# A two-layer graph network on one core: half of the zeroes begun in a later stage, one attention tile loaded earlier, and count masks spread over nine steps

## The chip, the cores and the metric

The kernel runs as one launch on one core of one Trainium2 chip. The metric is the device time of a run in microseconds. Three runs of the kernel before took 3403.36, 3404.73 and 3406.10 us; the median is 3404.73 us. One more run was profiled.

## The reference

Input is `x` (1250 nodes by 768) and 20,000 edges `src`, `dst`. Two layers follow, each a sum of a graph attention, a performer attention and a small feed-forward part:

```python
xn = _layernorm(x, axis=-1)
x = x + _L0_gnn_ref(xn, edge_index, ...) + _L0_mix_ref(xn[None], ...)[0]   # 2 GAT layers; performer + MLP
x = x + _L0_ffn_ref(_layernorm(x, axis=-1)[None], ...)[0]                  # routed experts
xn = _layernorm(x, axis=-1)
x = x + _L1_gnn_ref(xn, edge_index, ...) + _L1_mix_ref(xn[None], ...)[0]
x = x + _L1_ffn_ref(_layernorm(x, axis=-1)[None], ...)[0]
```

The graph attention is `e = leaky_relu(a_src[src] + a_dst[dst])`, a maximum of `e` over the edges that enter a node, `exp(e - m[dst])`, and a sum of `h[src]` with these weights over the edges. The kernel turns the edge list into a dense matrix of counts (how many edges lead from node s to node d), since an edge can occur more than once. The performer's output is `(phi(q) @ (phi(k).T @ v)) / (phi(q) @ sum(phi(k)))`, times a projection `proj_w`, plus a bias.

## The kernel before

Tokens are cut into `NT` = 10 tiles of `TP` = 125 rows. Float32 products run as three passes (`y_lo*w_hi`, `y_hi*w_lo`, `y_hi*w_hi`). The program is a row of stages. A stage is a `Stage` with an `nc.Block()`: each engine has its own instruction list, and lists are ordered only by semaphores. At the end of a block all engines meet (in the norm stage this is line 247), then the stage's semaphores are cleared (L68) and all engines meet again (L69). Nothing of the next stage is issued before. The order within a list is the order in which the Python code writes it; there is no scheduler.

The stages that matter here, in order:

- `norm_stage`. Rows of `x` come in, are normalised twice and turned. SP (the DMA queue's engine) stores the normalised rows to `xn_d`. POOL waits for the last rows of `x` (L276, `x_ld[4]`), and then `edges.clear` (L135) issues 26 DMAs that write zeroes over two count matrices `adj0_d` and `adj1_d` in HBM: 13 for each, 12 with rows and a small one for spare cells. Each matrix has 1250 x 1250 float32 cells, 6.25 MB.
- `performer_stage` "perf0" (six pairs of heads). DVE also finds the count of each edge's cell beside its own work (`counted.count`, L182), and POOL adds the counts into the matrices by 160 indirect DMAs (`counted.add`, L200 to L216), in turn to `adj0_d` and `adj1_d`, so that each waits for the one two before it to land. The first waits until all zeroes have landed (`edges.cleared`, L206). The first weights of this stage are loaded in the norm stage; its next ones (`load_v(0)`, features, `load_qk(1)`) are issued by SP in the stage.
- `gat_project_stage` "gat00proj". In step t, PE turns tile t+1 of the rows, multiplies tile t in two halves of the columns (c = 0, 1; 18 matmuls each), and after each half turns one half tile of the counts (`turn_counts`, L1718), of which DVE makes a bfloat16 mask (`keep_mask`, L1900). q = 2s + c names the half tiles of matrix rows s, 20 in all. The sum of `adj0` and `adj1` for rows s is `add_counts(s)` on DVE (L1895). All turned things pass through two PSUM banks `tps` in turn: an entry of the list `turns` may be written only when the one two entries before it has been read by DVE (`wait_slot`, L1711). In step t the halves 2t-2 and 2t-1 are turned, and 18 and 19 behind the last step. SP stores tile t of `h` as soon as it is kept, and behind the last of these the whole mask in three pieces (L1674).
- `proj_stage` ("proj0" and, in layer 2, "proj1"). SP loads tile 0 of the attention's output, the six blocks of the projection's weights, tile 1, the bias, rows for tiles 0 and 1, then the other tiles (L1077 to L1088). PE turns tile 0 and tile 1, and only then multiplies tile 0 (`turn_tile`, L1118), block by block as ACT and DVE have split the weights. POOL adds the bias to the rows (L1211), which come in pieces of tiles 0-1, 2-4 and 5-9; DVE adds PE's product to that (L1255).

Of the kernel before, what the change touches and what calls it, by code (L numbers as in the profile page):

```python
# [21 lines left out]
NT = 10  # L22
# [94 lines left out]
class Edges:  # L117
# [17 lines left out]
    def clear(self, pool):  # L135
        for flat in self.adj_flat:
            for r0 in range(0, N, ROWS):
                rn = min(ROWS, N - r0)
                pool.dma_start(flat[r0 * N:(r0 + rn) * N].rearrange("(p a n) -> p a n", p=rn, a=2),
                               self.zero[0:rn, :].unsqueeze(1).to_broadcast([rn, 2, N // 2])).then_inc(self.cleared, 16)  # L140
                self.cleared_n += 16
            pool.dma_start(flat[N * N:N * N + EXTRA].rearrange("(a n) -> a n", a=1),
                           self.zero[0:1, 0:EXTRA]).then_inc(self.cleared, 16)
            self.cleared_n += 16
# [17 lines left out]
class EdgeCounts:  # L162
# [37 lines left out]
    def add(self, pool):  # L200
        edges, added, sets = self.edges, self.added, len(self.edges.adj_flat)
        pool.wait_ge(edges.cleared, edges.cleared_n)
# [15 lines left out]
def norm_stage(nc, ident, src, dst, lower, edges, eps, x_d, normed_d, gain_cols, shift_cols, yT, first, late):  # L218
# [6 lines left out]
    with Stage(nc, "norm") as S:  # L225
# [21 lines left out]
        with nc.Block() as block:  # L247
# [25 lines left out]
            def _(pool):  # L273
# [4 lines left out]
                edges.clear(pool)  # L278
# [730 lines left out]
def proj_stage(nc, name, ident, attn_d, w_d, bias_d, xn_d, x_d, sum_d, eps, gain, shift, yT, ahead=(), more_shift_d=None,  # L1009
# [19 lines left out]
    with Stage(nc, name) as S:  # L1029
# [34 lines left out]
        with nc.Block() as block:  # L1064
            @block.sync
            def _(sp):
# [10 lines left out]
                load_a(0)  # L1077
                for kb in range(KB):
                    load_w(kb)
                load_a(1)  # L1080
# [499 lines left out]
def gat_project_stage(nc, name, ident, x_d, k, act_kind, bias_d, w_d, heads, width, asrc_d, adst_d, h, a_s, a_d, rows_d,  # L1580
# [12 lines left out]
    with Stage(nc, name) as S:  # L1593
# [30 lines left out]

        turns = [("x", 0), ("x", 1)]
        for t in range(1, NT):
            turns += [("x", t + 1)] if t + 1 < NT else []
            turns += [("m", 2 * t - 2), ("m", 2 * t - 1)] if edges is not None else []
        turns += [("m", 2 * NT - 2), ("m", 2 * NT - 1)] if edges is not None else []
# [11 lines left out]
        with nc.Block() as block:  # L1641
# [69 lines left out]
            def _(pe):  # L1711
# [35 lines left out]
                for t in range(NT):  # L1747
# [6 lines left out]
                    for c in range(2):  # L1754
# [10 lines left out]
                        if edges is not None and t:  # L1765
                            turn_counts(2 * t - 2 + c)
                if edges is not None:
                    turn_counts(2 * NT - 2)
                    turn_counts(2 * NT - 1)
# [61 lines left out]
            def _(dve):  # L1831
# [86 lines left out]
                dve.wait_ge(att_ld, 64)  # L1918
                for t in range(NT):
# [7 lines left out]
                    if edges is not None and t >= 2:  # L1927
                        keep_mask(2 * t - 4)
                    if t >= 2:
                        terms(t - 2)  # L1930
                    if edges is not None and t:
                        add_counts(t - 1)
                        if t >= 2:
                            keep_mask(2 * t - 3)
# [4 lines left out]
                if edges is not None:  # L1939
                    keep_mask(2 * NT - 4)  # L1940
                    add_counts(NT - 1)
                    keep_mask(2 * NT - 3)
                terms(NT - 2)
                if edges is not None:
                    keep_mask(2 * NT - 2)
                    keep_mask(2 * NT - 1)
# [1937 lines left out]
```

## Time and profile before

| | before |
|---|---|
| median of three runs | 3404.73 us (3403.36 to 3406.10) |
| profiled execution, whole | 3403.53 us |
| its span (first to last instruction) | 3401.4 us |
| busy: PE / PEld / DVE / ACT / POOL | 84 / 74 / 69 / 43 / 16 % |
| norm stage to perf0 | 0 to 84 us |
| perf0 | 84 to 549 us |
| gat00proj | 549 to 690 us |
| proj0, first instruction on SP | 690.60 us |

The profile is of one execution. It gives busy times and start times per instruction, and for each idle time what ended it. POOLq and SPq are the sequencers of these engines: DMA issues and waits that take no time on the engine. The span leaves out what lies before the first and behind the last instruction, 2.1 us here.

### The profile page before, as it was taken

What the parts mean: (1) busy time and instruction counts of PE and PEld (TensorE: products, weight loads), DVE (VectorE), ACT (ScalarE), POOL (GpSimd) and SP (SyncE); (2) the same over time, 40 slices, a digit from 0 to 9 for tenths busy, and PEclk for the clock granted to TensorE, in tenths of its full rate; (3) what the DMA queues carried; (4) which work ended last, traced back from release to release, by engine and by line L of the source; (5) the groups of instructions that cost most, each with busy time, mean ns of one, the idle gap of its engine ahead of it and who ended that gap; (6) DMA issues with size and microseconds to landing.
All of it is one profiled execution on the core that took longest, in us unless ns stands there. A gap on an engine that the chain in (4) does not pass through costs nothing. (4 is left out here: it accounts for less than half of the span.)

```text
span 3401.4 us, 50787 instructions
## 1 busy us (share of the span) xinstructions
PE 2869.5 (84%) x17896; PEld 2528.3 (74%) x17896; DVE 2332.3 (69%) x4168; ACT 1460.6 (43%) x2436; POOL 530.0 (16%) x358
## 2 busy tenths in 40 slices
PE   1999997877999997887997599878999977887795
PEld 1999996766888997777896233247999977777794
DVE  4765642856842544998664888657788868998775
ACT  3464652222112332554243577521556522554345
POOL 2677783220000000000002300000000022000000
PEclk9999998988999998999998699979999988998897
DMA  8433326684213554523131311253311068213301
GB/s 263 84 51 57 47 22 155 215 206 111 67 44 87 174 165 118 140 67 84 29 75 48 80 42 43 55 165 119 77 41 51 23 174 224 76 46 79 85 21 47
DMA packets 254534, 319.48 MB, mean 94 GB/s; under 512 B 98467, under 2 KB 176804, under 8 KB 254206
## 3 DMA queue, kind: packets, MB, share of 16 engines
q1 hardware_dynamic: 176574, 272.11, 29.8%
q0 software_dynamic: 77760, 44.83, 6.5%
q8 instruction: 110, 1.80, 0.2%
q14 instruction: 90, 0.74, 0.1%
HBM read 236.35 MB, written 79.53 MB: 93 GB/s over the span
## 5 line engine op out<-in xcount | busy, mean ns | idle before, releaser
L210 POOL DMA_INDIRECT adj_d<-edge_val,edge_off x160 | 336.3, 2102 | 150.8 <-DMA adj_d<-edge_val,edge_off 59.2
L3274 DVE TENSOR_TENSOR expert_wgel<-expert_gel,expert_wps 128x417 f32<-128x417 f32 (+1 forms) x384 | 202.8, 584 | 57.0 <-PE expert_wps L3199 47.3
L2185 PE MATMUL gat00att_ops<-gat00att_h,gat00att_p 125*125 x1600 | 198.8, 280 | 50.4 <-DVE gat00att_p L2159 50.4
L2185 PE MATMUL gat10att_ops<-gat10att_h,gat10att_p 125*125 x1600 | 195.9, 279 | 47.1 <-DVE gat10att_p L2159 47.1
L2185 PEld LDWEIGHTS gat00att_ops<-gat00att_h,gat00att_p 125*125 125x125 f32 x1600 | 184.7, 190 | 64.6 <-issue 64.5
L2185 PEld LDWEIGHTS gat10att_ops<-gat10att_h,gat10att_p 125*125 125x125 f32 x1600 | 184.0, 192 | 59.1 <-issue 59.1
L3246 ACT ACTIVATE expert_gel<-expert_hps 128x417 f32<-128x417 f32 (+1 forms) x384 | 193.8, 519 | 63.7 <-DVE expert_wgel L3274 52.3
L596 PE MATMUL perf_wide<-y_lo,perf_qk_hi 128*128 128x416 f32 (+1 forms) x432 | 155.5, 360 | 44.6 <-DVE perf_qk_lo L780 44.0
L734 ACT ACTIVATE xn_room<-perf_wide,perf_lnm 125x384 f32<-125x384 f32 (+2 forms) x228 | 114.2, 622 | 158.5 <-PE perf_wide L620 85.6
L1358 PE MATMUL fc_ps<-y_lo,fc_w_hi 128*128 128x512 f32 (+1 forms) x432 | 154.6, 358 | 21.4 <-DVE fc_w_lo L1400 21.4
L1511 PE MATMUL fc_ops<-fc_w_hi,fc_x_lo 128*125 128x384 f32 x480 | 163.7, 341 | 7.1 <-DVE fc_w_lo L1563 7.1
L1511 PE MATMUL fc_ops<-fc_w_lo,fc_x_hi 128*125 128x384 f32 x480 | 163.3, 340 | 0.0
L1511 PE MATMUL fc_ops<-fc_w_hi,fc_x_hi 128*125 128x384 f32 x480 | 162.8, 339 | 0.0
L1358 PE MATMUL fc_ps<-y_hi,fc_w_lo 128*128 128x512 f32 (+1 forms) x432 | 155.0, 359 | 0.0
L1358 PE MATMUL fc_ps<-y_hi,fc_w_hi 128*128 128x512 f32 (+1 forms) x432 | 154.8, 358 | 0.0
L596 PE MATMUL perf_wide<-y_hi,perf_qk_lo 128*128 128x416 f32 (+1 forms) x432 | 153.6, 356 | 0.0
L596 PE MATMUL perf_wide<-y_hi,perf_qk_hi 128*128 128x416 f32 (+1 forms) x432 | 153.4, 355 | 0.0
L2106 ACT ACTIVATE gat00att_e<-gat00att_e,a_s 125x1250 f32<-125x1250 f32 x80 | 107.0, 1338 | 105.2 <-DVE gat00att_e L2144 105.0
L2106 ACT ACTIVATE gat10att_e<-gat10att_e,a_s 125x1250 f32<-125x1250 f32 x80 | 107.0, 1338 | 97.0 <-DVE gat10att_e L2144 96.8
L2943 POOL MEMSET first_z<- 3x1250 bf16 x2 | 2.2, 1136 | 906.2 <-POOLq L69 906.2
L3192 PE MATMUL expert_hps<-first_z,first_w 99*128 99x417 bf16 (+1 forms) x384 | 134.3, 353 | 9.6 <-SPq L3143 8.6
L3199 PE MATMUL expert_wps<-first_wp,first_spread 128*128 128x417 f16 (+1 forms) x384 | 134.7, 352 | 5.6 <-DVE expert_wgel L3274 5.6
(503 smaller groups left out, 8281.1 us busy)
## 6 DMA issues: line engine op xcount, KB each, us to landing
fc_w<-in_L_mix_fc_w SPq DMA_DIRECT2D x96, 384.0 KB
adj_d<-edge_zero POOLq DMA_DIRECT2D x22, 546.9 KB, 28.0
gat00proj_adj<-adj_d POOLq DMA_DIRECT2D x20, 546.9 KB, 8.2
edge_keys<-keys_d SPq DMA_DIRECT2D x20, 437.5 KB
gat00att_sh<-shift_d SPq DMA_DIRECT2D x16, 546.9 KB
sh<-shift_d SPq DMA_DIRECT2D x16, 546.9 KB
perf_w<-in_L_mix_qkv_w SPq DMA_DIRECT2D x18, 384.0 KB
perf_w<-in_L_mix_W_qkv SPq DMA_DIRECT2D x18, 384.0 KB
```

The lines of the kernel that those rows point to most:

```text
L210: edges.nc.gpsimd.indirect_dma_start(out=edges.adj_flat[u].rearrange("(n a) -> n a", a=1), out_offset=bass.IndirectOffsetOnAxis(ap=edges.o ...
L596: ins = pe.matmul(wide[:, c, 0:cn], qk_parts[wp][:, 1 - side, kb, :], y_parts[yp][:, kb, c0:c0 + cn], start=(kb == 0 and n == 0), stop=(kb ...
L734: act.activation(out, in_, ACT.Exp, bias=lnm[0:parts, 0:1], scale=scale).then_inc(exp_done, 1)
L1358: ins = pe.matmul(ps[:, u, c0:c0 + cn], wp[:, u, kb, :], yT[yp][:, kb, c0:c0 + cn], start=(kb == 0 and n == 0), stop=(kb == KB - 1 and n = ...
L1511: ins = pe.matmul(ops[0:TP, t % 4, c * 512:c * 512 + half], xp[:, u, rows], wp[:, u, c * half:(c + 1) * half], start=(k == 0 and n == 0), ...
L2106: act.activation(e[:, s % RING, :], e[:, s % RING, :], ACT.Exp, bias=a_s02[:, bass.ds(hd, 1), s]).then_inc(e_done, 1)
L2185: ins = pe.matmul(ops[0:TP, u, b, t * w:(t + 1) * w], p[:, s, (t0 + t) * TP:(t0 + t + 1) * TP], h[:, s, bass.ds(hd, 1), :], start=(s == 0 ...
L2943: nc.gpsimd.memset(first.z[len(NPART) * ER:ZK, u, :], 1.0).then_inc(first_set, 1)
L3192: pe.matmul(hps[:, q % 3, 0:cn], w1[0:ZK, u, j * 128:(j + 1) * 128], z[0:ZK, u, c0:c0 + cn], start=True, stop=True).then_inc(h_done, 1)
L3199: pe.matmul(wps[:, q % 3, 0:cn], spread[:, j, :], wp[:, u, c0:c0 + cn], start=True, stop=True).then_inc(w_done, 1)
L3246: act.activation(gel[:, q % 3, 0:cn], hps[:, q % 3, 0:cn], ACT.Gelu_apprx_tanh).then_inc(gel_done, 1)
L3274: dve.tensor_tensor(wgel[:, q % W, 0:cn], gel[:, q % 3, 0:cn], wps[:, q % 3, 0:cn], ALU.mult).then_inc(wgel_done, 1)
```

## The change

Three things are changed.

1. `clear` takes a list of matrices. The norm stage clears `adj_flat[0:1]`; `add` in perf0 begins with `edges.clear(pool, edges.adj_flat[1:])` and then waits for all zeroes.
2. In `proj_stage`, `load_a(1)` is issued before the six `load_w`. This holds for proj0 and proj1.
3. In gat00proj the 20 half tiles of the counts are dealt over steps 1 to 9 by a list `due`: two in each step and three in steps 4 and 7, none behind the last step. Sums of the two matrices move with them.

```diff
-    def clear(self, pool):
-        for flat in self.adj_flat:
+    def clear(self, pool, flats):
+        for flat in flats:
...
     def add(self, pool):
         edges, added, sets = self.edges, self.added, len(self.edges.adj_flat)
+        edges.clear(pool, edges.adj_flat[1:])
         pool.wait_ge(edges.cleared, edges.cleared_n)
...
-                edges.clear(pool)
+                edges.clear(pool, edges.adj_flat[0:1])
...
                 load_a(0)
+                load_a(1)
                 for kb in range(KB):
                     load_w(kb)
-                load_a(1)
...
+        due, halves = [[]], iter(range(2 * NT))
+        for t in range(1, NT):
+            due.append([next(halves) for _ in range(3 if t in (4, 7) else 2)])
...
-            turns += [("m", 2 * t - 2), ("m", 2 * t - 1)] if edges is not None else []
-        turns += [("m", 2 * NT - 2), ("m", 2 * NT - 1)] if edges is not None else []
+            turns += [("m", q) for q in due[t]] if edges is not None else []
...
                         if edges is not None and t:
-                            turn_counts(2 * t - 2 + c)
+                            for q in (due[t][1:] if c else due[t][0:1]):
+                                turn_counts(q)
                 if edges is not None:
-                    turn_counts(2 * NT - 2)
-                    turn_counts(2 * NT - 1)
                     pe.wait_ge(mask_kept, 2 * NT)
...
+                pending = []
                 for t in range(NT):
...
-                    if edges is not None and t >= 2:
-                        keep_mask(2 * t - 4)
+                    if edges is not None and pending:
+                        keep_mask(pending.pop(0))
                     if t >= 2:
                         terms(t - 2)
                     if edges is not None and t:
-                        add_counts(t - 1)
-                        if t >= 2:
-                            keep_mask(2 * t - 3)
+                        for q in due[t]:
+                            if q % 2 == 0:
+                                add_counts(q // 2)
+                        for q in pending:
+                            keep_mask(q)
+                        pending = list(due[t])
+                        if len(pending) > 2:
+                            keep_mask(pending.pop(0))
...
-                if edges is not None:
-                    keep_mask(2 * NT - 4)
-                    add_counts(NT - 1)
-                    keep_mask(2 * NT - 3)
                 terms(NT - 2)
                 if edges is not None:
-                    keep_mask(2 * NT - 2)
-                    keep_mask(2 * NT - 1)
+                    for q in pending:
+                        keep_mask(q)
                 terms(NT - 1)
```

On POOL, the zeroes stand in the norm stage before the change (L139 and L142 are the DMAs of `clear`, L247 the end of the block, L210 the indirect adds of perf0):

```order
L139 DMA adj_d<-edge_zero 224x1x625 x11
L139 DMA adj_d<-edge_zero 36x1x625
L142 DMA adj_d<-edge_zero 16x1x8
L139 DMA adj_d<-edge_zero 224x1x625 x11
L139 DMA adj_d<-edge_zero 36x1x625
L142 DMA adj_d<-edge_zero 16x1x8
L247 UNCONDITIONAL_BRANCH
L68 ISA
L490 UNCONDITIONAL_BRANCH
L210 DMA adj_d<-edge_val,edge_off 1562628x1 x160
```

And on POOL after the change (its lines are numbered one higher there):

```order
L139 DMA adj_d<-edge_zero 224x1x625 x11
L139 DMA adj_d<-edge_zero 36x1x625
L142 DMA adj_d<-edge_zero 16x1x8
L248 UNCONDITIONAL_BRANCH
L68 ISA
L491 UNCONDITIONAL_BRANCH
L139 DMA adj_d<-edge_zero 224x1x625 x11
L139 DMA adj_d<-edge_zero 36x1x625
L142 DMA adj_d<-edge_zero 16x1x8
L211 DMA adj_d<-edge_val,edge_off 1562628x1 x160
```

Thirteen of the 26 zero DMAs have moved behind the end of the norm stage and stand directly before the first add.

On DVE in gat00proj, steps 4 and 5 before the change (L1869 is `low`, L1904 `keep_mask`, L1838 and L1843 `terms`, L1897 `add_counts`):

```order
L1869 TENSOR_TENSOR gat00proj_xT_lo<-gat00proj_tps,gat00proj_xT_hi 128x750
L1904 TENSOR_SCALAR gat00proj_mask<-gat00proj_tps 125x5x125
L1838 TENSOR_TENSOR gat00proj_prod<-gat00proj_h,gat00proj_att 125x1024 x2
L1843 TENSOR_REDUCE a_s<-gat00proj_prod 125x8
L1843 TENSOR_REDUCE a_d<-gat00proj_prod 125x8
L1897 TENSOR_TENSOR gat00proj_adj<-gat00proj_adj 125x1250
L1904 TENSOR_SCALAR gat00proj_mask<-gat00proj_tps 125x5x125
L1869 TENSOR_TENSOR gat00proj_xT_lo<-gat00proj_tps,gat00proj_xT_hi 128x750
L1904 TENSOR_SCALAR gat00proj_mask<-gat00proj_tps 125x5x125
```

And the same steps on DVE after the change (lines two higher):

```order
L1871 TENSOR_TENSOR gat00proj_xT_lo<-gat00proj_tps,gat00proj_xT_hi 128x750
L1906 TENSOR_SCALAR gat00proj_mask<-gat00proj_tps 125x5x125
L1840 TENSOR_TENSOR gat00proj_prod<-gat00proj_h,gat00proj_att 125x1024 x2
L1845 TENSOR_REDUCE a_s<-gat00proj_prod 125x8
L1845 TENSOR_REDUCE a_d<-gat00proj_prod 125x8
L1899 TENSOR_TENSOR gat00proj_adj<-gat00proj_adj 125x1250 x2
L1906 TENSOR_SCALAR gat00proj_mask<-gat00proj_tps 125x5x125 x2
L1871 TENSOR_TENSOR gat00proj_xT_lo<-gat00proj_tps,gat00proj_xT_hi 128x750
L1906 TENSOR_SCALAR gat00proj_mask<-gat00proj_tps 125x5x125
```

Step 4 has one sum and one mask more. The mask behind the second L1871 is of half 7 now; it was of half 6 before. On PE the five transposes of `gat00proj_adj` that close steps 4 and 7 have become ten, and the fifteen that close step 9 have become five.

## Rows read from the trace of the kernel before

**Rows 1.** Window: PE, PEld, DVE, ACT, POOL busy us, clock, DMA share, GB/s

```profile
58.00:82.00 24.00, 0.00 (x0) 0.00 (x0) 0.00 (x0) 0.00 (x0) 0.00 (x0) 1.00 0.82 261
93.00:112.00 19.00, 17.43 (x92) 16.60 (x90) 16.88 (x39) 14.90 (x20) 16.56 (x8) 1.00 0.17 3
```

**Rows 2.** Line 247, end of the norm block: durations ns, first and last start

```profile
L247 POOLq DRAIN  x1: 46819/46819/46819, 36.7 to 36.7; - x1
```

**Rows 3.** Timeline of POOL: start us, us, engine line op, idle before and releaser

```profile
24.94 7.99 POOL L139 DMA_DIRECT2D adj_d<-edge_zero  x12 [20.73 <-DMA xn_room<-in_x]
...
93.31 2.13 POOL L210 DMA_INDIRECT adj_d<-edge_val,edge_off  x1 [51.24 <-DVE edge_off L198]
```

**Rows 4.** DMA queues from 24.9 to 58.5 us: packets, MB, share of 16 engines

```profile
q0 software_dynamic: 1488, 6.43, 59.4%
q1 hardware_dynamic: 2205, 5.04, 43.0%
```

**Rows 5.** DMA queues from 79 to 81 us

```profile
q0 software_dynamic: 49, 0.12, 17.1%
```

**Rows 6.** Timeline of DVE, first split of perf0 and split of its value weights

```profile
84.42 0.96 DVE L778 CAST perf_qk_hi<-perf_w 128x1536 fp32r<-128x1536 f32 x1 [29.24 <-PEq L69]
...
108.75 1.30 DVE L778 CAST perf_v_hi<-perf_w 128x1536 fp32r<-128x1536 f32 x1
```

**Rows 7.** Timeline of SP, a weight load and the last store of perf0

```profile
111.87 0.97 SPq L501 DMA_DIRECT2D perf_w<-in_L_mix_qkv_w  x2
...
544.16 0.57 SPq L101 DMA_DIRECT2D attn_d<-perf_o  x1
```

**Rows 8.** Timeline of POOL, an add behind that load, the last add, the next stage

```profile
123.23 2.29 POOL L210 DMA_INDIRECT adj_d<-edge_val,edge_off  x1 [7.23 <-DMA adj_d<-edge_val,edge_off]
...
527.18 1.99 POOL L210 DMA_INDIRECT adj_d<-edge_val,edge_off  x1 [0.30 <-issue]
549.15 0.24 POOL L1693 MEMSET gat00proj_h<- 125x80 f32 x1 [19.98 <-POOLq L69]
```

**Rows 9.** Timeline of PE in gat00proj, second mask turn of step 4, first of step 5

```profile
618.51 0.71 PE L1725 MATMUL gat00proj_tps<-ident,gat00proj_adj 125*125 125x125 f32 x5
...
623.90 0.71 PE L1725 MATMUL gat00proj_tps<-ident,gat00proj_adj 125*125 125x125 f32 x5
```

**Rows 10.** Timeline of DVE in gat00proj, steps 4 and 5

```profile
611.11 1.46 DVE L1897 TENSOR_TENSOR gat00proj_adj<-gat00proj_adj 125x1250 f32<-125x1250 f32 x1
614.55 0.94 DVE L1869 TENSOR_TENSOR gat00proj_xT_lo<-gat00proj_tps,gat00proj_xT_hi 128x750 fp32r<-128x750 f32 x1 [1.27 <-ACT gat00proj_xT_hi L1796]
...
616.13 2.35 DVE L1838 TENSOR_TENSOR gat00proj_prod<-gat00proj_h,gat00proj_att 125x1024 f32<-125x1024 f32 x2
...
620.89 1.46 DVE L1897 TENSOR_TENSOR gat00proj_adj<-gat00proj_adj 125x1250 f32<-125x1250 f32 x1
```

**Rows 11.** Timeline of SP at the end of gat00proj

```profile
670.42 0.94 SPq L100 DMA_DIRECT2D mask_d<-gat00proj_mask  x1
...
685.23 0.51 SPq L1680 DMA_DIRECT2D rows_d<-gat00proj_rows  x1
690.60 0.33 SPq L100 DMA_DIRECT2D proj_a<-attn_d  x1
```

**Rows 12.** Timeline of PE in proj0, second and third turned tile

```profile
705.26 1.51 PE L1129 MATMUL proj_tps<-ident,proj_a 125*128 125x125 f32 x6 [9.68 <-DMA proj_a<-attn_d]
...
714.38 0.81 PE L1129 MATMUL proj_tps<-ident,proj_a 125*128 125x125 f32 x6
```

**Rows 13.** Timeline of POOL and DVE in proj0

```profile
710.25 3.65 POOL L1211 TENSOR_TENSOR proj_h<-proj_h,proj_bias 125x768 f32<-125x768 f32 x2 [38.16 <-DMA proj_h<-xn_d]
...
747.49 10.86 POOL L1211 TENSOR_TENSOR proj_h<-proj_h,proj_bias 125x768 f32<-125x768 f32 x5 [16.71 <-DMA proj_h<-xn_d]
...
750.73 0.95 DVE L1255 TENSOR_TENSOR proj_h<-proj_h,proj_hps 125x768 f32<-125x768 f32 x1 [1.46 <-PE proj_hps L1149]
```

**Rows 14.** Timeline of DVE in proj1, third tile's sum

```profile
2790.88 0.95 DVE L1255 TENSOR_TENSOR proj_h<-proj_h,proj_hps 125x768 f32<-125x768 f32 x1 [0.88 <-POOL proj_h L1211]
```

## Prediction

> **What bounds the kernel now.** I read the windows by engine first, then the places where all engines stand still, and only then the busy shares. From 58 to 82 us every engine is at 0.00 busy and the DMA share is 0.82 [rows 1]: that gap is the largest one the change touches. What holds it is in the rows of the norm block's end: POOL's drain lasts 46.8 us, from 36.7 to 83.5 [rows 2], while the zero queue q0 is still moving its last 0.12 MB between 79 and 81 us [rows 5]. DVE's first instruction of perf0 follows at 84.42 and its 29.24 us of idle time are put down to the barrier L69 [rows 6]. So the norm stage ends when POOL's zeroes have landed, about 1 us after the last packet.
>
> perf0 ends by SP: its last store is issued at 544.16 and the next stage begins at 549.15 [rows 7, 8]. POOL's last add is issued at 527.18, takes 1.99 us and had then 19.98 us until the next stage [rows 8]. So POOL has some 17 us to spare against SP's store and its landing (549.15 - 1.1 for the barrier = 548.0, against some 531.0 when the last add has landed: 1.99 us of issue and about as much until it lands).
>
> gat00proj goes by PE until step 9, and then by SP: the mask is stored from 670.42 on, behind the last tile of `h`; SP is through at 685.23, where it issues `rows_d`, and the next stage begins at 690.60 [rows 11]. proj0 and proj1 start by PE waiting for tile 1, and their middle goes by the transfers of rows, which POOL waits for [rows 12 to 14].
>
> **Part 1, the zeroes.** In the norm stage POOL issues 13 DMAs instead of 26, from 24.94 on [rows 3]. Up to 58.5 us q0 has moved 6.43 MB and q1 5.04 MB [rows 4]; one matrix is 6.25 MB, and the first one's descriptors stand ahead of the second's. So its bytes are through at about 58 us, as before. Before the change, 0.12 MB of 12.5 still came at 79 to 81 us and the drain ended at 83.5, 4.5 us behind the full flow; half the stream has half to all of that lag: the drain ends between 60.3 and 62.5 us. I take 62.0, near the upper end, since the row stores share the engines until then. DVE's first instruction of perf0 comes 0.9 us later, as before: 62.8 instead of 84.42, a start earlier by 21.6 us (bounds 21 and 23.3).
>
> Everything on PE, ACT and DVE in perf0 moves by that, if no weight comes late. The next weights are split by DVE 24.3 us after the stage's start [rows 6]. They are issued within some 4 us of it, and 1.5 MB of such loads beside the zeroes need, at q1's rate in rows 4 (5.04 MB in 33.6 us, 0.15 MB/us), 10 us. The cover is 10 us wide, so I cost it at nothing. SP's last store then is through at 548.0 - 21.6 = 526.4.
>
> POOL now has 13 DMAs more ahead of its adds. The last adds' way: issue from 62.7 on; first bytes some 2 us later; 6.25 + 1.5 MB at 342 GB/s (6.43 + 5.04 MB in 33.6 us [rows 4]) are 22.7 us; a lag of 3 to 4.5 us. That is 91.4 +- 2, and the first add about 1 us later, 92.4 instead of 93.31 [rows 3]. Then the 160 adds take what they took, 531.0 - 93.3 = 437.7 us. One of their stalls, 7.23 us at 123.23, follows SP's loads of 111.87 [rows 7, 8]; these are issued at 90.3 now, before the first add, and can't stall one. So POOL is through at 92.4 + 437.7 - 7.2 = 522.9 if the stall is gone, and at 530.1 if another load takes its place. The stage ends by the later of POOL and SP: 526.4 to 530.1, for 548.0. I take 528.0, the middle: **-20.0 us** (bounds -14, where zeroes land 4 us later and the stall stays, and -23.3).
>
> **Part 2, tile 1 ahead of the weights.** In proj0 PE turned tile 1 at 705.26 and then began to multiply tile 0; it reached tile 2 at 714.38 [rows 12]. Tile 1 comes first now, and the last weights with it by 705.3, since the same bytes have then arrived. Five of six blocks are multiplied by then. Splitting the last takes ACT and DVE about 0.9 us each and its six matmuls some 1.5 us: PE is at tile 2 at 708.9, 5.5 us earlier. But tile 2 stands in the queue behind the rows that POOL got at 710.25 [rows 13] and lands about 1.5 us later, at 711.8. So PE goes on 714.38 - 711.8 = 2.6 us earlier, less 0.7 for turning at the lower clock after the wait: 1.9. Then the row transfers take over: POOL gets rows 5 to 9 at 747.49, as before, needs 10.86 / 5 = 2.2 us for the first, and DVE, which added tile 5 at 750.73, can't do so before 749.6 [rows 13]. What is left is **-1.1 us** (bounds 0 and -2.6). In proj1 DVE's third sum waited for POOL at 2790.88 already [rows 14], and POOL's rows come when they came: **0** (bounds +0.5 and -1).
>
> **Part 3, the masks.** The last step's tail on PE and DVE gets shorter, but SP's mask store hangs on the last tile of `h` and takes 14.8 us by itself (685.23 - 670.42), so the tail was covered [rows 11]. What counts is when PE ends step 9. Ten more transposes stand before that: 0.55 us for five [rows 9], twice, 1.1 us. The larger term is a new wait by the two-bank rule. In step 4, DVE's second sum and third mask (1.4 + 0.7 us) fill the 2.05 us between its sum at 611.11 and its next `low` at 614.55, so DVE comes to that point at 615.4, 0.8 us later [rows 10]. Its next mask is half 7 now, which PE turns only at 618.51 [rows 9]; before it was half 6. DVE waits until 619.1, then keeps it (0.8), does `terms` (4.8, from 616.13 to 620.89), the sum (1.4) and half 8 (0.7): 626.9. In step 5 PE wants to turn half 9 into half 8's bank at 623.90 (the row before the change) and must wait until 626.9: +3.0 us, the transposes included. Between the two such steps DVE catches up, since its round there is shorter than PE's, and at steps 7 and 8 the same comes again. Sum **+6.0 us** (bounds +1.1, transposes alone, and +8).
>
> **Sum.** -20.0 - 1.1 + 0 + 6.0 = -15.1 us. The profiled execution took 3403.53 us, its span 3401.4, and so would take 3388.4; the median of the runs, 1.2 us higher, gives 3389.6. The forecast is 3389.5 us.
>
> **A rule weighed.** In the norm stage POOL issued its first 12 zero DMAs in 7.99 us, 0.67 us each [rows 3], beside a busy DVE. In perf0 they stand beside DVE's copies again. The Trainium skill, "SBUF — State Buffer", section "SBUF: two separate sides", says that DVE in a two-port mode locks GpSimd out, so that it can't write descriptors; it gives 620 ns alone and 3100 ns beside a copy. By that ratio the 12 issues would take, as an estimate, 40 us instead of 8, and the first add would come some 20 us later than I have it, POOL would be through at 550 and the time would be 3411.7. The row of the norm stage speaks against it.
>
> **Rivals.** (a) *The masks cost only their transposes.* If DVE is further ahead than I have it, or the bank is free in time, part 3 is +1.1: 3404.7 - 20.0 - 1.1 + 1.1 = 3384.7. For it: DVE idles 1.27 us a step [rows 10]. Against it: half 7 isn't there before 618.51. (b) *POOL's adds end perf0 late.* If the second matrix's zeroes need as long as they did beside the row stores (24.94 to 62.0, 37 us, instead of 29) and the stall stays, POOL is through at 530.1 + 8 = 538: part 1 is -10, the time 3399.6. For it: the same engines carry weights. Against it: those are 1.5 MB, the row stores and loads were 5.04. (c) *Slower: DVE starves POOL's issues.* The place is POOL's queue head in perf0. From 93 to 112 us DVE is busy for 16.88 of 19.0 us [rows 1]. If POOL could write only in DVE's gaps (11% of the time), 8 us of issue would need 72, the zeroes would have landed at some 138 us, and POOL would be through at 138 + 437.7 = 576, 28 us behind the old end: 3404.7 + 28 - 1.1 + 6.0 = 3437.6. It is slower than before from a first add later than 93.3 + 17 - 4.9 = 105.4 us on. The rule above names this mechanism.
>
> **How the numbers follow.** Chances: forecast 0.50, (a) 0.24, (b) 0.20, (c) 0.04, something unseen 0.02. The range reaches from the best bound of part 1 with (a), 3404.7 - 23.3 - 2.6 + 1.1 = 3379.9, to about (b), 3399. A measurement tells 0.2%, 6.8 us, from no change. Faster by more (under 3397.9): forecast, (a) and the lower two fifths of (b), less a rest, 0.83. Within 0.2%: the rest of (b) and some of the unseen, 0.12. Slower: 0.05.
>
> **What would show it.** Right: POOL's drain at the norm block's end is over at 60 to 62.5; DVE's first split in perf0 at 61 to 63.5; the first add near 92; gat00proj about 4 to 7 us longer from its first instruction to proj0's, with PE waiting for `gat00proj_mask` in steps 5 and 8; proj0 shorter by 1 us, proj1 by nothing. Wrong: a drain that ends near 83 all the same; a first add later than 96; no wait for the mask in step 5; a mask store that starts before the last tile of `h`.

## The result, and the profile after

| | before | after |
|---|---|---|
| median, 14 runs each | 3400.81 us (3396.18 to 3408.58) | 3388.71 us (3383.97 to 3398.02) |
| ratio, with its 95% interval | | 0.9967 (0.9958 to 0.9976) |
| profiled execution, span | 3401.4 us | 3381.8 us |

The kernel is faster by 11 us, 8 to 14 by the interval. The forecast was 3389.5 us. The two profiles are 19.6 us apart, more than the medians, so they hold some chance; what belongs to the change has to be told by stage. I take a stage's length from POOL's clear of semaphores (L68) that ends the stage before it to its own.

| stage | before | after | difference |
|---|---|---|---|
| norm | 80.8 | 59.4 | -21.4 |
| perf0 | 464.7 | 469.6 | +4.9 |
| gat00proj | 141.3 | 149.4 | +8.2 |
| proj0 | 108.8 | 101.1 | -7.7 |
| proj1 | 104.7 | 103.6 | -1.1 |
| all others, unchanged | | | -2.4 (single ones from -3.6 to +2.8) |

**Part 1.** First the end of the norm block, by line (durations in ns, first and last start in us). It answers to [rows 2]:

```profile
L248 POOLq DRAIN  x1: 31383/31383/31383, 30.7 to 30.7; - x1
```

The drain is over at 62.1 us; before it was at 83.5. The timeline of POOL in perf0 answers to [rows 3, 8] (start, us, line, what, idle time before it and its releaser):

```profile
63.44 7.78 POOL L139 DMA_DIRECT2D adj_d<-edge_zero  x12 [29.73 <-POOLq L69]
92.06 2.91 POOL L211 DMA_INDIRECT adj_d<-edge_val,edge_off  x1 [20.33 <-DMA adj_d<-edge_zero]
...
522.27 1.99 POOL L211 DMA_INDIRECT adj_d<-edge_val,edge_off  x1 [0.30 <-DMA adj_d<-edge_val,edge_off]
532.65 0.24 POOL L1696 MEMSET gat00proj_h<- 125x80 f32 x1 [8.39 <-POOLq L69]
```

Twelve zero DMAs were issued in 7.8 us beside a busy DVE, the first add came at 92.06, the last at 522.27. The forecast had the first add at 92.4. But POOL's adds do not end this stage; SP's stores do, behind PE and DVE. The timeline of DVE answers to [rows 6]:

```profile
62.98 0.96 DVE L779 CAST perf_qk_hi<-perf_w 128x1536 fp32r<-128x1536 f32 x1 [7.71 <-PEq L69]
...
92.01 0.96 DVE L779 CAST perf_v_hi<-perf_w 128x1536 fp32r<-128x1536 f32 x1 [6.02 <-DMA perf_w<-in_L_mix_qkv_w]
```

The first split is 21.4 us earlier. The value weights, though, are split 29.0 us after it and not 24.3, because DVE stood 6.02 us for their DMA. The timeline of SP shows the same from the other end, and answers to [rows 7]:

```profile
65.76 1.33 SPq L502 DMA_DIRECT2D perf_w<-in_L_mix_qkv_w  x2
67.14 11.56 SPq L514 DMA_DIRECT2D perf_feat<-in_L_mix_w_orf  x2
...
527.66 0.57 SPq L101 DMA_DIRECT2D attn_d<-perf_o  x1
```

SP needed 11.56 us to get two DMAs of features issued. Its last store went out 464.7 us after DVE's first split; before, 459.7. The DMA queues from 70 to 84 us, while zeroes and weights both had work, tell why (packets, MB, share of the 16 engines):

```profile
q0 software_dynamic: 938, 4.10, 91.6%
q1 hardware_dynamic: 945, 0.48, 11.3%
```

q0 has zeroes, most of them in packets of 5000 bytes; q1 has the value weights, in packets of 512 bytes (0.79 MB in 1536 packets). The two queues had the same number of packets through, and the weights so had an eighth of the bytes of the zeroes.

PE's clock fell as well. It stood for 7.05 us until DVE had split the weights (before, 1.54 us at this place) and began again at 94.91; before the change, at 111.99. Windows of the changed kernel, then of the kernel before (busy us of PE, PEld, DVE, ACT, POOL; granted clock; DMA share; GB/s):

```profile
92.00:95.00 3.00, 0.09 (x1) 0.12 (x1) 2.96 (x3) 0.00 (x0) 2.91 (x1) 0.60 0.04 12
95.00:100.00 5.00, 5.00 (x26) 5.00 (x27) 4.77 (x9) 4.27 (x6) 4.34 (x2) 0.56 0.84 215
```
```profile
112.00:117.00 5.00, 5.00 (x42) 5.00 (x43) 4.78 (x9) 4.28 (x6) 3.70 (x2) 1.00 0.78 205
```

The granted clock was 0.56 (1.0 is 2.4 GHz, 0.5 is 1.2 GHz) in the first 5 us behind the stand, with 26 matmuls begun or under way for 42 before the change.

**Part 2.** The timelines of PE and POOL in proj0, whose first instruction on SP is at 682.27, answer to [rows 12, 13]:

```profile
685.97 2.82 PE L1130 MATMUL proj_tps<-ident,proj_a 125*128 125x125 f32 x12 [19.06 <-DMA proj_a<-attn_d]
...
699.46 0.86 PE L1130 MATMUL proj_tps<-ident,proj_a 125*128 125x125 f32 x6 [1.20 <-DMA proj_a<-attn_d]
```
```profile
698.07 3.61 POOL L1212 TENSOR_TENSOR proj_h<-proj_h,proj_bias 125x768 f32<-125x768 f32 x2 [34.16 <-DMA proj_h<-xn_d]
```

Tiles 0 and 1 are turned at once. PE comes to tile 2 at 17.2 us after the stage's start, which is SP's first instruction in it (before at 23.8), and waits there 1.20 us for its landing. POOL has its first rows at 15.8 us (before at 19.7).

**Part 3.** The waits of PE in gat00proj, from its timeline, and SP's end of the stage, which answers to [rows 11]:

```profile
599.01 0.78 PE L1728 MATMUL gat00proj_tps<-ident,gat00proj_adj 125*125 125x125 f32 x5 [0.84 <-DVE gat00proj_mask L1906]
...
605.49 0.83 PE L1739 MATMUL gat00proj_tps<-ident,gat00proj_x 125*128 125x125 f32 x6 [0.45 <-DVE gat00proj_mask L1906]
...
612.36 0.78 PE L1728 MATMUL gat00proj_tps<-ident,gat00proj_adj 125*125 125x125 f32 x5 [1.85 <-DVE gat00proj_mask L1906]
...
645.91 0.78 PE L1728 MATMUL gat00proj_tps<-ident,gat00proj_adj 125*125 125x125 f32 x5 [1.86 <-DVE gat00proj_mask L1906]
```
```profile
661.46 0.31 SPq L100 DMA_DIRECT2D h_d<-gat00proj_h  x1
...
662.25 0.95 SPq L100 DMA_DIRECT2D mask_d<-gat00proj_mask  x1
...
676.13 0.91 SPq L1683 DMA_DIRECT2D rows_d<-gat00proj_rows  x1
682.27 0.33 SPq L100 DMA_DIRECT2D proj_a<-attn_d  x1
```

The waits of 1.85 us stand in the steps behind the two with three halves, as forecast. The mask store still begins behind the last tile of `h` and takes 13.9 us (662.25 to 676.13), so the whole delay of that tile is paid.

### The profile page after: what moved, and what is told of

It is laid out like the page before. It is cut to its first block and busy times, and to the rows that moved or that the text cites. A ratio compares the mean times of both kernels' runs of the same rounds, so it can differ in the third digit from the quotient of the medians.

```text
span 3381.8 us, 50787 instructions
## 1 busy us (share of the span) xinstructions
PE 2867.4 (85%) x17896; PEld 2525.4 (75%) x17896; DVE 2332.7 (69%) x4168; ACT 1458.1 (43%) x2436; POOL 527.2 (16%) x358
## 5 line engine op out<-in xcount | busy, mean ns | idle before, releaser
L3250 ACT ACTIVATE expert_gel<-expert_hps 128x417 f32<-128x417 f32 (+1 forms) x384 | 193.8, 519 | 64.9 <-DVE expert_wgel L3278 53.5
L597 PE MATMUL perf_wide<-y_lo,perf_qk_hi 128*128 128x416 f32 (+1 forms) x432 | 154.7, 358 | 23.3 <-DVE perf_qk_lo L781 22.4
L2110 ACT ACTIVATE gat00att_e<-gat00att_e,a_s 125x1250 f32<-125x1250 f32 x80 | 107.0, 1338 | 103.3 <-DVE gat00att_e L2148 103.1
```

What stands on the lines that cost most here:

```text
L597: ins = pe.matmul(wide[:, c, 0:cn], qk_parts[wp][:, 1 - side, kb, :], y_parts[yp][:, kb, c0:c0 + cn], start=(kb == 0 and n == 0), stop=(kb ...
L2110: act.activation(e[:, s % RING, :], e[:, s % RING, :], ACT.Exp, bias=a_s02[:, bass.ds(hd, 1), s]).then_inc(e_done, 1)
L3250: act.activation(gel[:, q % 3, 0:cn], hps[:, q % 3, 0:cn], ACT.Gelu_apprx_tanh).then_inc(gel_done, 1)
```

## Experiments

All times are medians; a ratio is to the kernel before on the same chip, with its 95% interval. Two experiments on different chips are compared by their ratios.

**e1: part 1 alone.** Edit to the kernel before:

```diff
+        edges.clear(pool, edges.adj_flat[1:])      # at the head of add()
-                edges.clear(pool)
+                edges.clear(pool, edges.adj_flat[0:1])
```

> The kernel before with part 1 alone (second matrix cleared in perf0). Theory A: in perf0 the zeroes stand beside the loads of the value weights; the two kinds of queue share the DMA engines packet by packet, so the small packets of the weights (0.82 MB in 1180 packets, against 2.43 MB of zeroes in 624) come through only with the last zeroes, at 92 us. DVE splits them 29 us after the stage's start and not 24.3, PE stands for 5.5 us more, and this shows as a stage perf0 that is 5 us longer: norm -21.4, perf0 +5, together -16.5 us against the kernel before. Rival B: the 5 us of perf0 are chance of one profile (other stages without a change differ by up to 3.6 us between the two profiles): then -20 us, and DVE's split of the value weights comes at +24.3.

3384.43 us, ratio 0.9952 (0.9939 to 0.9965): 16.3 us faster. Norm -20.6, perf0 +4.9 (469.57). From DVE's timeline:

```profile
91.08 1.03 DVE L779 CAST perf_v_hi<-perf_w 128x1536 fp32r<-128x1536 f32 x1 [2.67 <-DMA perf_w<-in_L_mix_qkv_w]
```

That is 27.2 us after its first split at 63.90, again late, and SP's last store came 464.6 us after that split. The loss is real: A holds. But the weights were 2.9 us late here and 4.7 in the changed kernel, for the same loss; the clock fell in both (see the part on the prediction). In the four profiles without part 1 perf0 took 462.8 to 465.4 us, in the six that have it with all zeroes issued at once 468.1 to 470.3.

**e2: part 2 alone.**

```diff
                 load_a(0)
+                load_a(1)
                 for kb in range(KB):
                     load_w(kb)
-                load_a(1)
```

> The kernel before with part 2 alone (attention tile 1 ahead of the weights in both projection stages). Theory A (the term of the prediction): -1.1 us in proj0 and 0 in proj1, since the rows' transfers set the middle of the stage; the -7.7 us of proj0 between the two profiles are then mostly chance of the DMA rate (5.61 against 6.15 MB in the first 22 us). Theory B: the gain is real and belongs to the order: -6 to -8 us in proj0, -1 in proj1, time -7 to -9. In B the rows of the next pieces land 4 to 5 us earlier after the stage's start in this profile too (POOL's third base 30 us after it and not 34.4).

3395.29 us, ratio 0.9992 (0.9983 to 1.0002): the medians differ by 5.5 us, the ratio says 2.7 (-0.7 to +5.8). proj0 took 100.9 us in the profile, proj1 103.4. B's 7 to 9 us are outside the interval; A's 1.1 us are inside it, and so is no gain at all. Over all profiles see below.

**e3: part 3 alone.** The list `due` and what uses it, on the kernel before.

> The kernel before with part 3 alone (masks over steps 1 to 9). Theory A: PE waits for gat00proj_mask in the steps behind the two with three halves (1.85 us each), ten more transposes (1.1 us) and two waits of 0.45 us between them stand before the last tile of h, and the mask store hangs on that tile: gat00proj +7 to +8 us, and the time +7 to +8. Rival: part of the +8.2 us is chance, and the transposes alone count: +1.1 to +2.

3408.83 us, ratio 1.0024 (1.0014 to 1.0035): 8.2 us slower. gat00proj +6.8 (148.07). PE's waits in its profile, grouped, from 595 us to the stage's end (total us, times, longest):

```profile
PE gat00proj_tps L1727 <- DVE gat00proj_mask L1905: 6.0, 4, 1.9
...
PE gat00proj_tps L1738 <- DVE gat00proj_mask L1905: 0.9, 2, 0.4
```

A holds: 6.0 + 0.9 us of waits and 1.1 of transposes, against 0.7 us of waits for the mask in the same stretch before. Of the 6.0, one of 1.4 us stands in step 3, ahead of the steps with three halves.

**e4: parts 1 and 2, without 3.** The edits of e1 and e2 together.

> The changed kernel without its part 3. If the parts add, it is faster than the changed kernel by what part 3 costs: 7 to 8 us (about 3380 where the changed kernel takes 3388). If part 3 costs its transposes alone, 1 to 2 us faster. If the gain of proj0 needs part 3 (another phase of the stage), proj0 takes 108 to 109 us here as in the kernel before, and the time is about that of the changed kernel.

3379.80 us, ratio 0.9943 (0.9931 to 0.9956), 8.9 us under the changed kernel. The parts add up: -16.3 - 2.7 + 8.2 = -10.8 for a measured -11.2 (by ratios), and proj0 took 104.3 us and not the 108 to 109 that it should have if its gain hung on part 3.

**e5: e4, with the second matrix's zeroes in two lots.**

```diff
             for i, r0 in enumerate(range(0, N, ROWS)):
+                if pause is not None and i == 6:
+                    pool.wait_ge(*pause)            # (w_ld, 32): the value weights
```

> Parts 1 and 2 (as e4_zeroes_tile, which took 3379.8 us), but in perf0 POOL issues only the first 6 zero DMAs at once and the other 7 when the first load of value weights has landed. Theory A: the 4.6 to 4.9 us that perf0 was longer come from these weights, which land only with the last zeroes. Now they land by some 15 us after the stage's start, DVE splits them at +24.3 us as in the kernel before and not at +29, and perf0 is 3 to 4.6 us shorter than in e4_zeroes_tile (469.3), unless POOL's adds, which begin 1 to 3 us later, end it. Time 3375 to 3377. Rival B: the longer perf0 comes from the adds (they wait for each other beside more loads): then the split moves but perf0 stays at 469 to 471.

3377.20 us, ratio 0.9933 (0.9919 to 0.9948). e4 had 0.9943, and the intervals overlap, so it is the trace and not the time that tells. Timelines of POOL, DVE (first split at 59.84) and SP:

```profile
60.29 3.91 POOL L141 DMA_DIRECT2D adj_d<-edge_zero  x6 [27.05 <-POOLq L69]
79.67 3.83 POOL L141 DMA_DIRECT2D adj_d<-edge_zero  x6 [15.47 <-DMA perf_w<-in_L_mix_qkv_w]
...
95.50 2.13 POOL L213 DMA_INDIRECT adj_d<-edge_val,edge_off  x1 [10.68 <-DMA adj_d<-edge_zero]
...
521.40 1.99 POOL L213 DMA_INDIRECT adj_d<-edge_val,edge_off  x1 [0.30 <-issue]
526.88 0.24 POOL L1696 MEMSET gat00proj_h<- 125x80 f32 x1 [3.49 <-POOLq L69]
```
```profile
83.79 0.96 DVE L781 CAST perf_v_hi<-perf_w 128x1536 fp32r<-128x1536 f32 x1
```
```profile
518.93 0.70 SPq L101 DMA_DIRECT2D attn_d<-perf_o  x1
```

DVE splits the value weights at +24.0 us without a wait, PE's granted clock stays at 1.00 there, and SP's last store is out at +459.1, as before the change (+459.7). So the late weights, with the fall of the clock behind them, were the whole loss on that path. SP's long issue of the features was not: it took 10.2 us here too. perf0 is 2.3 us shorter (467.0) and not 4.9: POOL's adds now end the stage. They begin 35.7 us after DVE's first split, where the changed kernel had 29.1 and I had allowed for 1 to 3 us more; POOL had 4.9 us to spare (8.39 of idle time before the next stage, now 3.49). What rival (b) of the prediction said, that POOL's adds end perf0, is so in this kernel, at a smaller price than it gave.

**e6: the changed kernel, three halves in steps 8 and 9.**

```diff
-            due.append([next(halves) for _ in range(3 if t in (4, 7) else 2)])
+            due.append([next(halves) for _ in range(3 if t in (8, 9) else 2)])
```

> The changed kernel (3388.7 us) with three halves in steps 8 and 9 instead of 4 and 7. Theory A: each step with three halves costs PE its wait for the bank in the step behind it (1.85 us), 0.45 us between two turns and 0.55 us for five transposes; in step 9 the wait behind it no longer stands before the last tile of h. gat00proj is then 3 to 4 us longer than before the change and not 8, the time 3384 to 3385. Rival: the cost is the delay of the sums and masks as a whole, wherever the third half stands: still +7 to +8, time 3388.

3379.48 us, ratio 0.9934 (0.9920 to 0.9948): 11 us under the changed kernel by the ratios (0.9967 there), and not to be told from e4 (0.9943). The forecast of 3384 was too cautious. PE's timeline in steps 8 and 9:

```profile
638.98 1.25 PE L1728 MATMUL gat00proj_tps<-ident,gat00proj_adj 125*125 125x125 f32 x10
...
644.25 0.71 PE L1728 MATMUL gat00proj_tps<-ident,gat00proj_adj 125*125 125x125 f32 x5
```

No wait stands behind step 8, though it has three halves. What differs may be the tile of rows: none is left to turn in step 9, and so DVE has no `low` to do. That is argued from the order of the lists and was not tried alone. Of part 3's cost nothing is left but 0.6 us for five transposes.

**e8: e6, and the mask stored in the course of the stage.**

```diff
                     for t in range(NT):
                         sp.wait_ge(h_kept, t + 1)
                         move_rows(sp, h_d[...], h[:, t]..., h_st)
-                    for s0, s1 in ((0, 5), (5, 9), (9, 10)):
+                        if t in (6, 8, 9):
+                            s0, s1 = {6: (0, 5), 8: (5, 8), 9: (8, 10)}[t]
```

> As e6_masks_at_end, and SP stores the mask's tiles 0 to 4 behind tile 6 of h, tiles 5 to 7 behind tile 8 and only tiles 8 and 9 at the end. Theory: the end of gat00proj hangs on SP's 14 us of mask stores, which start behind the last tile of h; that is why nothing came of finishing the masks earlier. With most of them stored before, the stage ends by the rows (last mask, last terms, a transpose, their store): some 8 to 10 us shorter than e6_masks_at_end, time 3374 to 3377. Rival: the early stores hold up the tiles of h or the loads of the counts in the middle (they share the queue of SP and the DMA engines): gain under 3 us.

3372.04 us, ratio 0.9915 (0.9899 to 0.9931), 7.4 under e6 on the same chip; gat00proj 133.8 for 142.4. SP's timeline:

```profile
625.38 0.36 SPq L100 DMA_DIRECT2D mask_d<-gat00proj_mask  x1
...
654.77 0.32 SPq L100 DMA_DIRECT2D h_d<-gat00proj_h  x1
...
658.83 0.33 SPq L100 DMA_DIRECT2D mask_d<-gat00proj_mask  x1
...
664.32 0.32 SPq L1683 DMA_DIRECT2D rows_d<-gat00proj_rows  x1
667.03 0.33 SPq L100 DMA_DIRECT2D proj_a<-attn_d  x1
```

The next stage begins 12.3 us after the last tile of `h` was stored, and not 20.8 (661.46 to 682.27). So the store behind that tile did set the end, which is why finishing the masks earlier gave nothing in part 3.

**e9: PE's order instead of the transfers'.** Loads as before; PE turns tile 1 behind the product of tile 0.

```diff
                     if t + 1 < NT:      ->   if 0 < t < NT - 1:
                         turn_tile("a", t + 1)
...
                     ins.then_inc(h_done, 1)
+                    if t == 0:
+                        turn_tile("a", 1)
```

> The kernel before, loads in their old order, but in both projection stages PE turns attention tile 1 only behind the product of tile 0. It tells apart what part 2 gave. Theory A (PE's order): PE no longer stands idle for tile 1 and reaches tile 2 when it has landed, at 18.8 to 21 us after proj0's start and not at 21.1 to 23.8: about -2 us in proj0, half of what part 2 gave. Theory B (the transfers themselves): part 2 also made tile 2 (17.2 against 18.8 us) and the first rows (15.6 to 16.4 against 17.2 to 19.5 us) land earlier; these stay late here, so POOL's first base is at 17.4 us or later. Both can hold; if PE's order were all, this kernel would gain as much as e2_tile_alone (about 5 us).

3401.00 us, ratio 1.0000 (0.9986 to 1.0013): no gain that can be seen. proj0 104.5, proj1 104.4. The timelines of PE and POOL (the stage starts at 690.24):

```profile
709.96 0.86 PE L1129 MATMUL proj_tps<-ident,proj_a 125*128 125x125 f32 x6 [1.97 <-DMA proj_a<-attn_d]
```
```profile
708.75 3.60 POOL L1213 TENSOR_TENSOR proj_h<-proj_h,proj_bias 125x768 f32<-125x768 f32 x2 [37.20 <-DMA proj_h<-xn_d]
```

PE comes to tile 2 at 19.7 us by waiting for its landing, and POOL has the first rows at 18.5. In the changed kernel these were 17.2 and 15.8. So PE's order alone does not bring the landings forward. In time e9 and e2 can't be told apart, since their intervals overlap.

**e10: e4 with e8's early stores** (masks in their old places).

> Parts 1 and 2 with the masks in their old places (18 and 19 behind the last step), and SP's early mask stores as in e8_masks_stored_early (3372.0 us, gat00proj 133.8 us). It asks what spreading the masks is worth once the mask stores no longer end the stage. Theory A: next to nothing. The end hangs on DVE's last terms and their transpose, which came 131.7 us after the stage's start before the change and 130.6 in e8: gat00proj 134 to 136 us, time 3372 to 3375. Rival B: the two late masks hold back the last piece of the store, and the stage ends by it: 138 us or more, time 3376 or more.

3376.54 us, ratio 0.9924 (0.9910 to 0.9937); gat00proj 137.1. The stage lies between the two forecasts, the time at the edge of B's. Two rows of PE's timelines, of e8 and of this kernel:

```profile
663.60 0.40 PE L1775 MATMUL gat00proj_tps<-ident,a_s 125*80 125x125 f32 x1 [8.87 <-DVE a_d L1845]
```
```profile
668.34 0.40 PE L1774 MATMUL gat00proj_tps<-ident,a_s 125*80 125x125 f32 x1 [10.07 <-DVE a_d L1844]
```

Counted from the clear before the stage that is 131.1 and 134.4 us. With the store out of the way, having no masks behind the last step is worth 3.3 us of the stage in these profiles and 3.1 us by the ratios (0.9915 and 0.9924), whose intervals overlap.

**e11: e8 with 9 and 4 zero DMAs.** As e5's edit, with `i == 9`, on e8.

> e8_masks_stored_early (3372.0 us) with the zeroes of perf0 in two parts, 9 zero DMAs at once and the last 4 when the value weights have landed (e5_zeroes_in_two had 6 and 7; there SP's path was back at its old length, but POOL, whose last add was issued at 521.4, ended the stage at 526.3). Theory: POOL's first add comes 2 to 4 us earlier than in e5 (32 to 34 us after the stage's start and not 36), the weights still land within DVE's 24 us of cover; perf0 takes 464.5 to 466 us and not 467.0 or 469 to 470, time 3367 to 3369. Rival: with 9 DMAs ahead the weights land after 24 us all the same and perf0 stays at 467 to 468: 3370.

3365.59 us, ratio 0.9893 (0.9880 to 0.9907), the lowest median of all. But its theory fell: perf0 took 469.7 us in the profile. Rows of POOL, DVE and PE, then windows (busy us of PE, PEld, DVE, ACT, POOL; granted clock; DMA share; GB/s):

```profile
86.84 2.10 POOL L141 DMA_DIRECT2D adj_d<-edge_zero  x3 [19.22 <-DMA perf_w<-in_L_mix_qkv_w]
...
97.76 2.14 POOL L213 DMA_INDIRECT adj_d<-edge_val,edge_off  x1 [8.31 <-DMA adj_d<-edge_zero]
```
```profile
86.58 0.96 DVE L781 CAST perf_v_hi<-perf_w 128x1536 fp32r<-128x1536 f32 x1 [1.69 <-DMA perf_w<-in_L_mix_qkv_w]
```
```profile
89.48 0.55 PE L580 MATMUL perf_wide<-perf_v_lo,y_hi 128*125 128x256 f32 x1 [2.68 <-DVE perf_v_lo L783]
```
```profile
89.00:93.00 4.00, 3.52 (x16) 3.55 (x17) 3.85 (x8) 2.98 (x5) 0.45 (x1) 0.50 0.98 209
93.00:98.00 5.00, 5.00 (x35) 5.00 (x34) 4.75 (x10) 4.71 (x7) 0.24 (x1) 0.74 1.02 274
```

DVE had the weights 25.3 us after its first split (61.30), 1.0 us later than before the change, and waited 1.69 us for them, PE 2.68; PE's granted clock was then 0.50 (1.2 GHz) in the next 4 us and 0.74 in the 5 behind them. SP's last store came at +464.8. The first add came later than in e5 (36.5 us after DVE's first split, for 35.7), not earlier.

**e12: e8 with 6 and 7.** e8 with e5's edit.

> e8_masks_stored_early with the zeroes of perf0 in two parts, 6 DMAs at once and 7 when the value weights have landed. With 9 and 4 (e11_best) the weights came 1.7 us after DVE wanted them, PE stood 2.7 us instead of 1.1, its granted clock then fell to 0.50 for some 6 us, and SP's last store of perf0 was issued 464.8 us after DVE's first split, as late as with all at once (463 to 465) and not at 459.1 as in e5_zeroes_in_two. Theory: here the weights are in time, no fall of the clock near 90 us, last store at 459 and perf0 467 (POOL ends it); norm, perf0, gat00proj together 1 to 3 us shorter than in e11_best (660 from the start of norm). Rival: the place of the pause doesn't matter within the noise of these stages: 3365.6 as e11_best.

3368.21 us, ratio 0.9900 (0.9882 to 0.9917). SP's last store at +458.9, perf0 466.0, POOL again the end, all as the theory has it; norm, perf0 and gat00proj together 658.3 for e11's 659.5. The time isn't lower than e11's all the same, and the three kernels e11 to e13 can't be told apart; nor can any of them from e8 (0.9915) beyond their intervals. In this profile proj0 took 108.1 and proj1 108.8, though both have part 2.

**e13: e12, with tile 2 ahead of the weights too.** `load_a(2)` moved behind `load_a(1)`.

> e12_early_and_two, and in both projection stages attention tile 2 is loaded ahead of the weights as well. With part 2, PE waits 0.8 to 1.6 us for tile 2 (landing 17 to 19 us after the stage's start). Theory A: that landing is what holds PE; with tile 2 early PE goes on by 1 to 3 us sooner at first, but POOL's rows for tiles 2 to 4 and 5 to 9 (30 and 52 us after the start) then set the pace: proj0 0 to 1.5 us shorter, 101.5 to 103. Rival B: weights and first rows come 1 to 2 us later for it, and the first product and sum with them: proj0 unchanged or up to 1 us longer.

3367.53 us, ratio 0.9902 (0.9886 to 0.9918); proj0 104.1, proj1 103.1: no gain that can be seen, and the first sum on DVE came 20.9 us after the start where other kernels with part 2 had it at 17.4 to 19.2. B is the nearer.

## Why the prediction was right, and where it wasn't

The time was right to 0.8 us (3389.5 against 3388.71), and that is luck in good part. The sum started from 3404.73 us, the median of three runs; fourteen runs put the kernel before at 3400.81, 3.9 us lower. The change itself was forecast at -15.1 us and measured at -11.2 (-8.2 to -14.3 by the interval), so its size was too large by some 4 us, and the base was too high by as much. By e1 to e3 the terms were:

| term | forecast (bounds) | measured alone |
|---|---|---|
| part 1 | -20.0 (-14 to -23.3) | -16.3 (-11.9 to -20.7) |
| part 2 | -1.1 (0 to -2.6; proj1 +0.5 to -1) | -2.7 (+0.7 to -5.8); medians -5.5 |
| part 3 | +6.0 (+1.1 to +8) | +8.2 (+4.8 to +11.9) |

**Part 1, the norm stage and POOL's way:** right. The drain ended at 62.1 (forecast 62.0), the first split was at 62.98 (62.8), the first add at 92.06 (92.4), the last was issued at 522.27. One stall did stay, of 5.89 us at 105.86: the loads that were to be issued at 90.3, ahead of the first add, had to wait for DVE's late split and went out at 94.8, behind it.

**Part 1, perf0: the step that failed** is "The cover is 10 us wide, so I cost it at nothing". I took q1's rate from [rows 4], where it moved 5.04 MB in 2205 packets, 2.3 KB each. The value weights go in packets of 512 bytes, and the row of 70 to 84 us shows that they had as many turns as the zeroes, not as many bytes. The trace of the kernel before had this already, from 32 to 40 us, where stores and zeroes moved side by side:

```profile
q0 software_dynamic: 422, 1.85, 59.7%
q1 hardware_dynamic: 422, 1.33, 42.8%
```

The Trainium skill states this, in "DMA: Bandwidth & Descriptors", section "Queues, rings and completion order": each DMA engine goes round the queues that have work, a packet at a time. A packet of that page holds several descriptors, and the profile's packets here are single rows, so the two counts are not of the same thing; but the shares agree with the trace (945 packets of the one beside 938 of the other), and I should have weighed it. At 945 packets in 14 us, an estimate, 1536 packets need 23 us; the first came at 67.9 us and the last at 91.6.

What the delay cost is more than DVE's wait, and this the forecast had nowhere. DVE split the value weights 4.7 us later after its first split than before the change; two splits on it was 6.4 us behind, since PE had worked at the lower clock in between. In all seven profiles with late weights (1.0 to 5.3 us later than before) PE stood 2.7 to 7.1 us, its granted clock fell to 0.50 for some 7 us, and SP's last store came 463.1 to 465.3 us after DVE's first split. In the seven with weights in time PE stood 1.1 to 1.6 us, the clock did not fall there, and the store came at 457.7 to 460.5. The loss hardly goes with how late the weights were: e11, with 1.0 us, lost as much as the changed kernel by the stage's end. e5 shows that the 5 us hang on this and nothing else on SP's side, and that the stage can't give all of them back, since POOL's end stood 4.9 us behind.

**The rule that I weighed** (DVE keeps GpSimd from writing descriptors) cost nothing more here than in the norm stage: 7.78 us for twelve issues in perf0, with DVE busy for 7.42 of them, beside 7.99 there [rows 3]. Rival (c) is out.

**Part 2: the term was mis-sized.** "Tile 2 [...] lands about 1.5 us later, at 711.8" took a landing from one profile. In that profile proj0 was a slow draw: four profiles without part 2 gave 108.8, 104.2, 107.4 and 104.5 us, the first of them being that one. Nine with it (all but e13) gave 100.9 to 104.3 and once 108.1, mean 103.4 against 106.2; proj1 has 104.7 against 105.5. So part 2 is worth about 3.6 us by the profiles, between the two figures of e2, with single profiles up to 5.5 us off their mean; a part of that size is likely but not clear of chance (e2's interval reaches past zero), and most of the -7.7 was chance. What I got wrong is the landings. I had tile 2 at 21.2 us after the start (711.8), and it was there at 17.2; I had the rows where they were, and they came earlier too. POOL's first were there 15.6 to 17.3 us after the start in the nine profiles with part 2 (mean 16.3), and 17.4 to 19.7 in the four without (mean 18.3); its last ones, for tiles 5 to 9, 51.4 to 54.0 us after the start with part 2 and 53.5 to 56.9 without. Why the same bytes land sooner in that order stays open; e9 shows only that it isn't PE's order.

**Part 3: right in mechanism, too small in size.** The waits are where they were forecast, in steps 5 and 8. I had counted 3.0 us for each step with three halves, all told. In PE's timeline steps 4 and 5 together took 4.4 us more than before and steps 7 and 8 3.2 more, since PE also waited 0.45 us between the mask's turn and the rows', and 0.84 before the first mask turn of step 4. That the covered tail gives nothing back was right, and e8 and e10 show it from both sides.

**Rivals.** (a) fell with e3 (5.5 us of waits in the steps with three halves and behind them). (b) didn't happen in the changed kernel, where POOL had 4.9 us to spare; e5 and e12 brought it about.

**The version that beats both:** e8's masks and stores, with the zeroes in two lots, 3365.6 to 3368.2 us, 1.0 to 1.1% under the kernel before; three times the gain of the change. It has parts 1 and 2 as well; e8, with all zeroes at once, had 3372.0 us, and what the two lots add to it is not clear of the intervals.

## What to carry to other kernels

A load that was covered alone was not covered here beside a bulk transfer on another queue: count its packets and theirs, not its bytes, and let the bulk wait for the load. The wait is not its whole price: look at PE's granted clock behind it. An engine that is done early gives nothing while a store stands behind another engine's last work: move the store first, then shorten what feeds it. And a landing time read from one profile moves by 2 us and a stage by 4 (proj0, 104.2 to 108.8 us with the same code), so a term of that size needs more than one profile, and the base that it is added to more than three runs (3404.73 us from three, 3400.81 from fourteen).

## What the runs showed of the hardware

- One queue's share of the DMA engines went by packets: from 70 to 84 us of the changed kernel 945 packets of mostly 512 bytes moved 0.48 MB beside 938 of mostly 5000 bytes that moved 4.10 MB, and before the change 422 stood beside 422 from 32 to 40 us. SP, which fed the queue of small packets, stood 11.56 us in the issue of two DMAs that took 2.2 us before the change, with no zeroes beside them.
- A stand of 2.68 us of PE (e11) was followed by a granted clock of 0.50 and 0.74 over 9 us, one of 7.05 (the changed kernel) by 0.50 from 93 to 99 us; stands of 1.11 us (e5) and 1.54 (before) at the same place by none below 1.00.
- Unchanged stages had two lengths: the stage behind the first layer's experts took 69.8 to 71.1 us in some profiles and 73.2 to 73.4 in others, perf1 377.5 to 378.2 or 380.5 to 381.7. Nothing in the kernels goes with it.
